# Two-layer recurrent and windowed attention kernel, 16 sequences on one core: the rounded part and the rest of a chunk's decays stacked in one operand, and three steps between stages put elsewhere

## The chip, the cores and the metric

The kernel runs on one core of one Trainium2 chip. The metric is the device time of one execution in microseconds. The kernel before takes 3458.81 us (median of three runs, 3458.78 to 3458.85).

## The reference, cut to what matters

The input is 16 sequences of 1024 tokens with 256 features. Each passes through two layers: `x = x + attention(norm(x)) * silu(ffn(norm(x)))`. The first layer has a gated linear attention (16 heads of 16) and a mixture of 8 experts of which the best 2 count; the second has a windowed attention (64 keys) and a ternary feed-forward network of 1024 hidden units.

The change is in the first attention. Its recurrence is

```python
gk = (jax.nn.log_sigmoid(x @ Wgk1 @ Wgk2 + bgk2) / 16.0).reshape(Bb, Ll, H, Dh)
def step(state, inp):
    qt, kt, vt, gt = inp
    gate = jnp.exp(gt)
    state = state * gate[..., None] + vt[..., None] * kt[..., None, :]
    out_t = jnp.einsum('bhvk,bhk->bhv', state, qt)
    return (state, out_t)
```

The kernel computes it in chunks of 128 tokens, so for each chunk it needs running sums of `gk`, counted from the middle of the chunk (position 64), and the totals of the chunk's first and second half.

## The kernel before, in words

A sequence is 8 chunks of 128 tokens (NC = 8) and two groups of 512 (NG = 2). The 16 sequences are unrolled in one block; each engine runs its own list of instructions in the order of the program and waits on semaphores. `at(name, value)` is a count within the current sequence. A sequence takes some 212 us and goes through these stages:

- **Head.** The head of the next sequence (norm, turned x, low-rank gate input, gate pre-activations) is computed during the feed-forward stage of the current one. `head_rstd` on GpSimd (L367) computes a reciprocal root for four chunks; it waits for `nve_ok`, which VectorE signals after `head_moments`. `head_normalise` on VectorE (L372) follows, and TensorE turns two chunks with `head_turn`.
- **Decays.** ScalarE computes Exp and then Ln of the pre-activations (L890, L899); VectorE forms `gk` for two chunks (L1194) and rounds it to float32r, `gk_hi` (L1198); GpSimd's `decay_low` (L804) subtracts to get the rest, `gk_lo`. TensorE's `cumulate(c)` (L1576, L1577) multiplies three constant 128 by 128 matrices with both parts: six products of 256 columns per chunk, in float32r, which keeps the sums exact enough. `cumulate(0)` stands between `first_queries_keys(6)` and `(7)`; `cumulate(c + 1)` stands in chunk c between `experts_up(c, 1)` and the products with the state (L1713). ScalarE's `decays(c)` takes three Exp of the sums (L924, L928, L933). `parity_scores(c)` on TensorE (L1619) waits for the last of them.
- **SP's queue.** SyncE loads x (8 transfers, L744, after the outputs of the sequence before have landed), then for each group writes the gate rows to DRAM (L749), waits until they have landed, and loads them back spread over 128 partitions as `g_wide` (L755, two transfers of 512 KB).
- **GpSimd's queue.** `parity_queries(0)`, the four `decay_low`, then `hidden_gated(0)` (L819), which waits for `g_wide`, then for each chunk the mask of the state (L839), `parity_queries(c + 1)` (L776) and `hidden_gated(c + 1)`. TensorE's `experts_up(c, 0)` (L1647) waits for `hidden_gated(c)`.
- **Chunks of the first attention.** Per chunk: scores (L1619), values and gates (L1508), `experts_up` (L1647, L1650), `cumulate(c + 1)`, then, after VectorE's masked scores (`causal_scores`, L1245), the products of L1713 and L1719, the turned output, the state's product (L1733) and, in chunks 0 to 3, `experts_down` (L1549).
- **Windowed attention.** Per chunk: masks (L1768), scores (L1781), turned probabilities (L1798), values (L1816), their turn (L1825). For parts 2 and 3 `window_values` on TensorE (L1756) reuses a bank half that VectorE's `attention_bias` (L1415) reads, and waits for it. VectorE's order is row maxima (L1378), shifted scores (L1387) for each of four score banks, then `attention_bias(c - 1)`, then `attention_out(c)`.
- **Feed-forward.** 16 steps n: products of L1879 and L1884, relu on ScalarE (L1113), the square on GpSimd (L867), rounding on ScalarE (L1092), the rest on VectorE (L1470), and `project(n - 3)` on TensorE (L1897), which waits for that rest. GpSimd's `head_rstd` follows its squares 4 and 7; VectorE's `head_normalise` runs in its steps 6 to 9.

## Time and profile before

| | |
|---|---|
| median of three runs | 3458.81 us |
| the profiled execution's own time | 3460.7 us |
| its span | 3459.0 us |
| TensorE matmul busy | 3342.5 us, 97% |
| VectorE, ScalarE, GpSimd busy | 75%, 54%, 37% |
| the chain that ended last: TensorE, VectorE, ScalarE, issue | 75%, 12%, 5%, 5% |
| mean granted TensorE clock | 0.997 |

The span runs from the first to the last instruction; the execution's own time is 1.7 us longer. "Issue" in the chain is time in which the engine waited for nothing that the profile shows. In a timeline, the bracket behind a row is the engine's idle time before it and who ended it; a row of the chain of waits has a start, a length and a name. Matmul ends in a timeline are modelled, so consecutive matmuls overlap by about 0.16 us there; starts are the better measure.

### The profile page before, as it was taken

To read this page: it belongs to the slowest core of one execution; us is meant where nothing else is said; L and a number is where in the kernel's file an instruction comes from. 1 tells how busy PE (TensorE), PEld (TensorE's weight loads), DVE (VectorE), ACT (ScalarE), POOL (GpSimd) and SP (SyncE) were. 2 spreads that over 40 slices of the span, in tenths; PEclk is the share of its full clock that TensorE was granted. 3 is DMA by queue.
4 is the path that set the end of the run, shared out by engine and by line. 5 is a ranking of instruction groups with operands and counts; after the bars stand their busy time and mean duration, and the time that the engine had idled before them with its cause. 6 is when DMAs were issued, how large, how long until landed. Compare 5 with 4: busy or idle time off the path is not lost.

```text
span 3459.0 us, 88576 instructions
## 1 busy us (share of the span) xinstructions
PE 3342.5 (97%) x34556; PEld 2274.0 (66%) x34556; DVE 2607.4 (75%) x6329; ACT 1863.8 (54%) x4135; POOL 1273.4 (37%) x1393
## 2 busy tenths in 40 slices
PE   6999999999999999999999999999999999999998
PEld 3676666766666666666666666666676666766666
DVE  6777867778677777877778777786777867778777
ACT  3364654646546465463655636456364653646546
POOL 4424244242442524325233342423434244242442
PEclk8999999999999999999999999999999999999999
DMA  4001010010110101011010100101001010010110
GB/s 105 18 22 47 24 38 19 24 44 24 38 23 24 40 24 47 14 38 26 24 50 11 50 18 20 49 12 49 18 23 45 24 38 23 20 44 24 38 23 26
DMA packets 98479, 109.59 MB, mean 32 GB/s; under 512 B 21153, under 2 KB 75025, under 8 KB 98065
## 3 DMA queue, kind: packets, MB, share of 16 engines
q1 hardware_dynamic: 93200, 102.25, 11.3%
q8 instruction: 276, 4.52, 0.5%
q10 hardware_dynamic: 4864, 1.69, 0.2%
q14 instruction: 139, 1.13, 0.1%
HBM read 74.01 MB, written 17.30 MB: 26 GB/s over the span
## 4 chain that ended last, share of the span: by engine, by line
PE 75%; DVE 12%; ACT 5%; issue 5%; POOL 1%; DMA 0%; DVEq 0%; SPq 0%; ACTq 0%; POOLq 0%
PE bank L1549 6%; PE bank L1508 5%; PE bank L1879 5%; PE bank L1647 5%; PE bank L1529 5%; PE bank L1781 5%; PE bank L1897 4%; PE bank L1719 4%; PE bank L1664 3%; PE bank L1619 3%; PE bank L1816 3%; PE bank L1842 3%; PE bank L1604 3%; PE bank L1713 2%; DVE am L1245 2%
## 5 line engine op out<-in xcount | busy, mean ns | idle before, releaser
L867 POOL TENSOR_TENSOR qx<-qx 128x512 f32<-128x512 f32 x256 | 277.3, 1088 | 658.7 <-ACT qx L1113 657.8
L1470 DVE TENSOR_TENSOR sq_lo<-qx,sq_hi 128x512 fp32r<-128x512 f32 x256 | 224.1, 875 | 177.1 <-ACT sq_hi L1092 176.6
L1378 DVE TENSOR_REDUCE row_max<-bank 128x4 f32<-128x384 f32 x512 | 270.8, 550 | 95.4 <-PE bank L1781 95.0
L1245 DVE TENSOR_TENSOR am<-bank,causal 128x512 f32<-128x512 f32 x512 | 328.1, 683 | 11.3 <-PE bank L1619 11.3
L988 ACT ACTIVATE tanh_g<-bank 128x256 f32<-128x256 f32 x128 | 49.3, 385 | 394.9 <-PE bank L1508 394.9
L1508 PE MATMUL bank<-w_vg,xt 128*128 128x512 f32 x512 | 252.3, 615 | 0.0
L1549 PE MATMUL bank<-xt,w_down 128*128 128x512 f32 x512 | 237.2, 596 | 0.0
L1897 PE MATMUL bank<-sq_hi,pj_t 128*128 128x512 f32 x512 | 213.2, 416 | 14.8 <-DVE sq_lo L1470 10.3
L1387 DVE TENSOR_TENSOR am<-bank,row_max 128x384 f32<-128x384 f32 x384 | 212.8, 554 | 9.8
L1113 ACT ACTIVATE qx<-bank,scale_fc 128x512 f32<-128x512 f32 x256 | 177.9, 695 | 70.9 <-PE bank L1884 69.0
L1032 ACT ACTIVATE am<-am 128x384 f32<-128x384 f32 x384 | 202.9, 528 | 8.5 <-DVE am L1387 8.5
L1897 PE MATMUL bank<-sq_lo,pj_t 128*128 128x512 f32 x512 | 202.7, 396 | 0.0
L776 POOL TENSOR_TENSOR qx<-qt,par_mask 128x512 f32<-128x512 f32 x128 | 136.3, 1065 | 164.7 <-ACT qt L453 148.4
L1092 ACT CAST sq_hi<-qx 128x512 fp32r<-128x512 f32 x256 | 159.0, 621 | 55.8 <-POOL qx L867 52.8
L1304 DVE TENSOR_TENSOR state_sum<-bank,state_mid 128x256 f32<-128x256 f32 x112 | 47.4, 423 | 176.5 <-PE bank L1733 176.5
L785 POOL TENSOR_SCALAR o_veps<-o_mom 128x1 f32<-128x1 f32 x128 | 38.0, 297 | 367.3 <-DVE o_mom L1325 367.3
L1879 PE MATMUL bank<-xh,fc_t 128*128 128x512 f32 x512 | 171.9, 416 | 0.0
L1781 PE MATMUL bank<-k,qt 32*32 32x192 f32 x8192 | 164.5, 332 | 4.6 <-ACT qt L966 4.6
L1798 PEld LDWEIGHTS bank<-ident,am 64*96 64x96 f32 x4096 | 130.1, 123 | 58.6 <-issue 26.9
L1798 PE MATMUL bank<-ident,am 64*96 64x64 f32 x4096 | 166.9, 221 | 0.0
L1619 PE MATMUL bank<-qx,k 32*128 32x256 f32 x2048 | 146.6, 400 | 15.4 <-issue 12.1
L1879 PE MATMUL bank<-xl,fc_t 128*128 128x512 f32 x512 | 159.9, 393 | 0.0
(264 smaller groups left out, 8671.4 us busy)
## 6 DMA issues: line engine op xcount, KB each, us to landing
g_wide<-gate_rows SPq DMA_DIRECT2D x64, 512.0 KB, 6.0
x<-in_L_attn_x SPq DMA_DIRECT2D x128, 128.0 KB, 2.3
qt<-in_L_attn_x SPq DMA_DIRECT2D x128, 128.0 KB, 2.6
out<-x SPq DMA_DIRECT2D x128, 128.0 KB, 1.7
k<-k SPq DMA_DIRECT2D x96, 128.0 KB, 2.4
qt<-in_L_attn_x ACTq DMA_DIRECT2D x8, 128.0 KB, 7.6
x<-in_L_ffn_w_fc SPq DMA_DIRECT2D x1, 1024.0 KB, 5.9
attn<-in_L_ffn_w_proj SPq DMA_DIRECT2D x1, 1024.0 KB, 8.7
```

The source lines that it names most:

```text
L867: nc.gpsimd.tensor_tensor(sq[:, n % 3, :], relu[:, n % 3, :], relu[:, n % 3, :], ALU.mult)\
L1245: nc.vector.tensor_tensor(am_tiles[:, :, j], bank[3 + j][:].rearrange("p (f e t) -> p f e t", f=2, e=2), causal[:].unsqueeze(1).unsqueeze( ...
L1378: nc.vector.tensor_reduce(row_max[:, j, :], bank[1 + j][:, 0:4 * KW].rearrange("p (h k) -> p h k", k=KW), AX.X, ALU.max, negate=(j == 0)). ...
L1387: nc.vector.tensor_tensor(pr[:, j], bank[1 + j][:, 0:4 * KW].rearrange("p (h k) -> p h k", k=KW), row_max[:, j, :].unsqueeze(2).broadcast_ ...
L1470: nc.vector.tensor_tensor(sq_lo[:, n % 3, :], sq[:, n % 3, :], sq_hi[:, n % 3, :].bitcast(F32), ALU.subtract)\
L1508: mm = nc.tensor.matmul(dst, xt[:, k, c * P:(c + 1) * P], w[:, k, :], start=(k == 0), stop=(k == KD - 1))
L1549: mm = nc.tensor.matmul(bank[5 if g else j][:], w_down[:, k, j * P:(j + 1) * P], xt[:, k, g * 512:(g + 1) * 512], start=(k == 0), stop=(k ...
L1619: mm = nc.tensor.matmul(bank[3 + j][:, half * 2 * P:(half + 1) * 2 * P], kt[rows, half, c * P:(c + 1) * P], qp[rows, c % 2, half], start=T ...
L1781: mm = nc.tensor.matmul(bank[1 + j][b * WB:(b + 1) * WB, t * 2 * KW:(t + 1) * 2 * KW], q2[rows, t, first:first + WB], k2[rows, :, first:fi ...
L1798: mm = nc.tensor.transpose(bank[5 + r][0:KW, h * QB:(h + 1) * QB], pr[rows, 2 * p + h // 4, h % 4, :], ident[rows, rows])
L1879: nc.tensor.matmul(h_bank, fc_t[:, k, m * P:(m + 1) * P], t[:, g, k, :], start=(t is xh and k == 0), stop=False)
L1897: mm = nc.tensor.matmul(bank[5 + o][:], pj_t[:, m, o * P:(o + 1) * P], part[:, n % 3, :], start=(m == 0 and part is sq_hi), stop=(m == MT ...
```

## The change

The two operands of `cumulate` are built anew. `gk_first` holds, for a chunk, the rounded decays of its first 64 tokens in partitions 0 to 63 and their rests in partitions 64 to 127; `gk_second` holds the rests of the second 64 tokens in partitions 0 to 63 and the rounded ones in 64 to 127. Three constant matrices stand in `cumulator`: one for the first half, one for the second, and all ones. The running sum is the first matrix with `gk_first` plus the second with `gk_second`; the half totals are all ones with either. That is four products per chunk instead of six.

To get there, VectorE still writes the rounded part into `gk_first` (all 128 partitions), GpSimd writes the rest into `gk_low` (the tile `xn`, where it wrote float32r into `xl` before), and three transfers from SBUF to SBUF per pair of chunks, issued by SyncE, move the halves (`decay_moves`): 64 partitions of 2 KB each, twelve per sequence. The third of a pair waits for the first to land. `decay_moves(0)` stands between the loads of x and the first gate rows, those for pairs 1 to 3 between the two groups' gate transfers. `cumulate(c)` waits for the transfers of its pair.

The other parts: ScalarE takes one Exp of a single column into a new tile `warm` between `experts_relu(2)` and `(3)`; VectorE's `attention_bias(c - 1)` stands ahead of the last row maximum for c = 1 and 2; GpSimd's `head_rstd` follows its squares 5 and 8 in place of 4 and 7; VectorE's `head_normalise` pairs run in steps 6, 7, 9 and 10 in place of 6 to 9. The constants' preparation on GpSimd before the first sequence changes with the matrices. Declarations of `warm`, `gk_low = xn` and the renamed constants, and two renamed uses of `gk_hi`, are left out of the diff below.

```diff
@@ -174,8 +175,8 @@
     xh = sb("xh", [P, NG, KD, 512], F32R)
     xl = sb("xl", [P, NG, KD, 512], F32R)
 
-    gk_hi = xh[:].rearrange("p g k t -> p (g k t)").rearrange("p (c d) -> p c d", d=D)
-    gk_lo = xl[:].rearrange("p g k t -> p (g k t)").rearrange("p (c d) -> p c d", d=D)
+    gk_first = xh[:].rearrange("p g k t -> p (g k t)").rearrange("p (c d) -> p c d", d=D)
+    gk_second = xl[:].rearrange("p g k t -> p (g k t)").rearrange("p (c d) -> p c d", d=D)
     q2 = qt
     x_next = qt[:].rearrange("p k t -> p (k t)").rearrange("p (c d) -> p c d", d=D)
     am_flat = am[:].rearrange("p h t -> p (h t)")
@@ -290,9 +292,10 @@
              "st2 ve2 rs2 xn2_ok xt2p_ok xt2_ok qk2p_ok qk2_ok low_ok kh_ok kd_ok v2p_ok v2_ok sc_ok max_ok sub_ok "
              "pr_ok ptp_ok pt_ok ptd_ok pv_ok oc_ok xp_ok rden_ok o2_ok o2tp_ok o2t_ok s2p_ok s2_ok xh_ok xl_ok tp_ok thi_ok tst_ok h2p_ok "
              "relu_ok sq_ok sqh_ok sql_ok pj_ok ft_ok ftp_ok tf2_ok f3_ok f4_ok y2_ok gkh_ok gkl_ok nst_ok nve_ok nrs_ok "
-             "nxn_ok hqp_ok hqk_ok").split()
+             "nxn_ok hqp_ok hqk_ok gkm_ok gkd_ok").split()
     s = {n: sem(n) for n in names}
     out_parts = (bank[6][:, 0:D], bank[1][:, D:2 * D])
+    normalise_steps = (6, 7, 9, 10)
     turn_steps = (MT + 2, MT + 3, MT + 5, MT + 6)
     pair_turn_banks = (2, 1, 3)
     turn_banks = {6: 7, 7: 0}
@@ -322,9 +325,9 @@
             (17, "top_ok"),
             (24, "pt_ok sub_ok"),
             (32, "gw_ok pr_ok am_ok max_ok at_ok sc_ok ptp_ok"),
-            (64, "gl_ok"),
+            (64, "gkm_ok gl_ok"),
             (96, "kd_ok"),
-            (128, "xc_ok"),
+            (128, "xc_ok gkd_ok"),
     ):
         per_sequence.update((name, count) for name in signals.split())
 
@@ -508,9 +511,9 @@
                 link(nc.gpsimd.affine_select(out=tile, in_=tile, compare_op=ALU.is_ge, fill=BIG, base=WIN - 1,
                                              pattern=[[-1, width]], channel_multiplier=1))
 
-            for t in (ident, second_half, xt2, k2, w_low, low_t, gates):
+            for t in (ident, cum_first, cum_second, xt2, k2, w_low, low_t, gates):
                 link(nc.gpsimd.memset(t[:], 0.0))
-            for t in (causal, first_half):
+            for t in (causal, all_ones):
                 link(nc.gpsimd.memset(t[:], 1.0))
             nc.gpsimd.memset(minus_half[:], -0.5).then_inc(cleared, 1)
             link(nc.gpsimd.affine_select(out=ident[:], in_=ident[:], compare_op=ALU.not_equal, fill=1.0, base=0,
@@ -521,11 +524,13 @@
                 head_rstd(pool, part)
             link(nc.gpsimd.affine_select(out=causal[:], in_=causal[:], compare_op=ALU.is_ge, fill=0.0, base=0,
                                          pattern=[[1, P]], channel_multiplier=-1))
-            link(nc.gpsimd.tensor_copy(cum_mid[:], causal[:]))
-            link(nc.gpsimd.tensor_scalar(cum_mid[0:QB, :], cum_mid[0:QB, :], -1.0, None, ALU.add))
-            link(nc.gpsimd.memset(first_half[QB:P, :], 0.0))
-            link(nc.gpsimd.memset(second_half[QB:P, :], 1.0))
-            for i, t in enumerate((cum_mid, first_half, second_half)):
+            link(nc.gpsimd.memset(cum_second[:, QB:P], 1.0))
+            for half in range(2):
+                rows = slice(half * QB, (half + 1) * QB)
+                for t, cols, fill in ((cum_first, slice(0, QB), -1.0), (cum_second, slice(QB, P), 0.0)):
+                    link(nc.gpsimd.affine_select(out=t[rows, cols], in_=t[rows, cols], compare_op=ALU.is_ge, fill=fill,
+                                                 base=0, pattern=[[1, QB]], channel_multiplier=-1))
+            for i, t in enumerate((cum_first, cum_second, all_ones)):
                 link(nc.gpsimd.tensor_copy(cumulator[:, i, :], t[:]))
             link(nc.gpsimd.memset(pick[:], 0.0))
             for r in (0, 2):
@@ -744,7 +749,24 @@
                         sp.dma_start(x[:, c, :], x_dram[bass.ds(seq * NC + c, 1), :, :].rearrange("o p d -> (o p) d"))\
                           .then_inc(s["xc_ok"], 16)
 
+                    def decay_moves(i):
+
+                        two, low, high = slice(2 * i, 2 * i + 2), slice(0, QB), slice(QB, P)
+                        sp.wait_ge(s["gkh_ok"], at("gkh_ok", i + 1))
+                        sp.dma_start(gk_second[high, two, :].bitcast(F32), gk_first[high, two, :].bitcast(F32))\
+                          .then_inc(s["gkm_ok"], 16)
+                        sp.wait_ge(s["gkl_ok"], at("gkl_ok", i + 1))
+                        if i:
+                            sp.wait_ge(s["gkd_ok"], at("gkd_ok", 32 * i))
+                        sp.dma_start(gk_second[low, two, :].bitcast(F32), gk_low[high, two, :]).then_inc(s["gkd_ok"], 16)
+                        sp.wait_ge(s["gkm_ok"], at("gkm_ok", 16 * (i + 1)))
+                        sp.dma_start(gk_first[high, two, :].bitcast(F32), gk_low[low, two, :]).then_inc(s["gkd_ok"], 16)
+
+                    decay_moves(0)
                     for g in range(NG):
+                        if g:
+                            for i in range(1, NC // 2):
+                                decay_moves(i)
                         sp.wait_ge(s["gx_ok"], at("gx_ok", g + 1))
                         sp.dma_start(gate_dram[g], gate_rows[8:8 + E, g * 512:(g + 1) * 512]).then_inc(s["gw_ok"], 16)
                         sp.wait_ge(s["gw_ok"], at("gw_ok", 16 * (g + 1)))
@@ -801,8 +823,8 @@
 
                     def decay_low(i):
                         pool.wait_ge(s["gkh_ok"], at("gkh_ok", i + 1))
-                        nc.gpsimd.tensor_tensor(gk_lo[:, 2 * i:2 * i + 2, :], gk[:, 2 * i:2 * i + 2, :],
-                                                gk_hi[:, 2 * i:2 * i + 2, :].bitcast(F32), ALU.subtract)\
+                        nc.gpsimd.tensor_tensor(gk_low[:, 2 * i:2 * i + 2, :], gk[:, 2 * i:2 * i + 2, :],
+                                                gk_first[:, 2 * i:2 * i + 2, :].bitcast(F32), ALU.subtract)\
                           .then_inc(s["gkl_ok"], 1)
 
                     def rstd2(part, lo, hi):
@@ -866,8 +888,8 @@
                             pool.wait_ge(s["sql_ok"], at("sql_ok", n - 2))
                         nc.gpsimd.tensor_tensor(sq[:, n % 3, :], relu[:, n % 3, :], relu[:, n % 3, :], ALU.mult)\
                           .then_inc(s["sq_ok"], 1)
-                        if n in (4, 7):
-                            head_rstd(pool, n // 7)
+                        if n in (5, 8):
+                            head_rstd(pool, n // 8)
                 now["copy"] = 0
 
             @block.scalar
@@ -915,6 +937,7 @@
                         act.wait_ge(s["gtp_ok"], at("gtp_ok", b + 1))
                         nc.scalar.copy(gate_rows[:, b * 512:(b + 1) * 512], bank[gate_banks[b]][32:64, :]).then_inc(s["gx_ok"], 1)
                     experts_relu(2)
+                    nc.scalar.activation(warm[:], gdiff[:, 0:1], ACT.Exp)
                     experts_relu(3)
                     def decays(c):
 
@@ -1427,9 +1450,11 @@
                         shifted(4 * c + 5)
                         maxima(4 * c + 6)
                         shifted(4 * c + 6)
+                        if 0 < c < 3:
+                            attention_bias(c - 1)
                         maxima(4 * c + 7)
                         shifted(4 * c + 7)
-                        if c:
+                        if c >= 3:
                             attention_bias(c - 1)
                         attention_out(c)
                         if c < 3:
@@ -1479,9 +1504,10 @@
                                 head_stats(dve, c)
                         if n == 3:
                             head_moments(dve)
-                        if 6 <= n < 10:
-                            head_normalise(dve, 2 * (n - 6))
-                            head_normalise(dve, 2 * (n - 6) + 1)
+                        if n in normalise_steps:
+                            p = normalise_steps.index(n)
+                            head_normalise(dve, 2 * p)
+                            head_normalise(dve, 2 * p + 1)
                         if n == NG * MT - 2:
                             head_low_split(dve, 1)
                     finish2(3)
@@ -1566,15 +1592,17 @@
                     experts_down(3)
                     def cumulate(c):
 
-                        pe.wait_ge(s["gkl_ok"], at("gkl_ok", c // 2 + 1))
+                        pe.wait_ge(s["gkd_ok"], at("gkd_ok", 32 * (c // 2 + 1)))
                         if c == 0:
                             pe.wait_ge(s["qk_ok"], at("qk_ok", 3))
                             pe.wait_ge(s["hr_ok"], at("hr_ok", 4))
                         else:
                             pe.wait_ge(s["am_ok"], at("am_ok", 4 * c - 2))
-                        for i, out in enumerate((bank[3][:, 0:D], bank[4][:, 0:D], bank[4][:, D:2 * D])):
-                            nc.tensor.matmul(out, cumulator[:, i, :], gk_hi[:, c, :], start=True, stop=False)
-                            mm = nc.tensor.matmul(out, cumulator[:, i, :], gk_lo[:, c, :], start=False, stop=True)
+                        first, second = gk_first[:, c, :], gk_second[:, c, :]
+                        nc.tensor.matmul(bank[3][:, 0:D], cumulator[:, 0, :], first, start=True, stop=False)
+                        nc.tensor.matmul(bank[3][:, 0:D], cumulator[:, 1, :], second, start=False, stop=True)
+                        nc.tensor.matmul(bank[4][:, 0:D], cumulator[:, 2, :], first, start=True, stop=True)
+                        mm = nc.tensor.matmul(bank[4][:, D:2 * D], cumulator[:, 2, :], second, start=True, stop=True)
                         mm.then_inc(s["cum_ok"], 1)
 
                     first_queries_keys(6)
```

## Rows read from the trace of the kernel before

**Rows 1.** The page's chain that ended last, by engine.
```profile
PE 75%; DVE 12%; ACT 5%; issue 5%; POOL 1%; DMA 0%; DVEq 0%; SPq 0%; ACTq 0%; POOLq 0%
```

**Rows 2.** Chain of waits, start of the seventh sequence's first attention: start us, us, what.
```profile
1346.87 0.12 PE bank L1576
...
1349.31 0.75 issue
```

**Rows 3.** Timeline of SyncE's queue, same stretch: start us, us, operation.
```profile
1337.49 3.66 SPq L744 DMA_DIRECT2D x<-in_L_attn_x  x8
1342.10 0.29 SPq L749 DMA_DIRECT2D gate_rows<-low_t  x1
1343.72 1.28 SPq L755 DMA_DIRECT2D g_wide<-gate_rows  x2
```

**Rows 4.** The page's DMA issues: size, median us from issue to landing.
```profile
x<-in_L_attn_x SPq DMA_DIRECT2D x128, 128.0 KB, 2.3
...
k<-k SPq DMA_DIRECT2D x96, 128.0 KB, 2.4
```

**Rows 5.** Timelines of GpSimd and TensorE, same stretch.
```profile
1351.25 1.28 POOL L819 TENSOR_TENSOR qx<-qx,g_wide 128x512 f32<-128x512 f32 x1 [4.62 <-DMA g_wide<-gate_rows]
...
1353.17 1.89 PE L1647 MATMUL bank<-w_up,qx 128*128 128x256 f32 x8
```

**Rows 6.** Timelines of SyncE, GpSimd, TensorE where the fourteenth sequence starts its first attention.
```profile
2829.42 1.28 SPq L755 DMA_DIRECT2D g_wide<-gate_rows  x2
...
2837.05 1.27 POOL L819 TENSOR_TENSOR qx<-qx,g_wide 128x512 f32<-128x512 f32 x1 [5.79 <-DMA g_wide<-gate_rows]
...
2838.37 1.99 PE L1647 MATMUL bank<-w_up,qx 128*128 128x256 f32 x8 [0.43 <-POOL qx L819]
```

**Rows 7.** Windows, fourteenth and fifteenth sequence: us, busy per engine, PEclk, DMA, GB/s.
```profile
2834.67:3047.37 212.70, 207.59 (x2155) 141.02 (x2155) 160.51 (x389) 115.62 (x258) 77.81 (x82) 1.00 0.12 31
3047.37:3259.33 211.96, 207.27 (x2154) 140.98 (x2155) 160.51 (x388) 115.59 (x258) 77.79 (x82) 1.00 0.12 30
```

**Rows 8.** Timeline of TensorE's weight loads in chunk 1; groups by line, whole span.
```profile
1365.95 0.52 PEld L1713 LDWEIGHTS bank<-qt,state_mid 128*128 128x128 f32 x4 [0.20 <-DVE am L1245]
...
L1713 PEld LDWEIGHTS bank<-qt,state_mid 128*128 128x128 f32 x512 | 67.2, 190 | 26.8 <-DVE am L1245 25.9
```

**Rows 9.** Timeline of ScalarE, same stretch as Rows 2.
```profile
1347.51 1.28 ACT L924 ACT_TABLE_LOAD   x1
1348.81 0.39 ACT L924 ACTIVATE decay_in<-bank 128x256 f32<-128x256 f32 x1
```

**Rows 10.** Timelines of TensorE and VectorE in the windowed attention.
```profile
1246.22 0.65 PE L1756 MATMUL bank<-ident,low_t 64*96 64x64 f32 x8 [0.28 <-DVE attn L1415]
...
1245.75 0.41 DVE L1415 TENSOR_TENSOR attn<-bank,bc_o 128x256 f32<-128x256 f32 x1
...
1248.34 1.02 DVE L1378 TENSOR_REDUCE row_max<-bank 128x4 f32<-128x384 f32 x2 [0.41 <-PE bank L1781]
```

**Rows 11.** Timelines of GpSimd and TensorE in the feed-forward stage.
```profile
1294.11 1.40 POOL L367 TENSOR_TENSOR rstd<-veps,minus_half 128x4 f32<-128x4 f32 x1 [3.35 <-DVE veps L361]
1295.47 2.04 POOL L867 TENSOR_TENSOR qx<-qx 128x512 f32<-128x512 f32 x2
...
1294.43 0.63 PE L1879 MATMUL bank<-xh,fc_t 128*128 128x512 f32 x2
...
1296.52 0.62 PE L1879 MATMUL bank<-xh,fc_t 128*128 128x512 f32 x2
...
1299.15 0.62 PE L1879 MATMUL bank<-xh,fc_t 128*128 128x512 f32 x2
```

**Rows 12.** Windows in the kernel's prologue; columns as in Rows 7.
```profile
51.70:53.70 2.00, 0.00 (x0) 0.00 (x0) 0.00 (x0) 2.00 (x4) 0.00 (x0) 1.00 0.00 0
53.80:56.10 2.30, 0.00 (x0) 0.00 (x0) 0.00 (x0) 0.56 (x3) 0.01 (x1) 0.50 0.03 7
56.20:60.50 4.30, 4.30 (x5) 1.79 (x6) 2.84 (x13) 2.72 (x6) 0.94 (x1) 0.50 0.75 193
```

More of the change, by code:

```diff
@@ L113, in build_program @@
     gden = sb("gden", [P, NC])
+    warm = sb("warm", [P, 1])
     g_top = sb("g_top", [P, 2, NC])
@@ L205, in build_program @@
     z, zact, gk = am_flat.rearrange("p (c d) -> p c d", d=D), xn, attn2
+    gk_low = xn
     u_nat = am_flat[:, 0:MT * RANK].rearrange("p (m r) -> p m r", m=MT)
@@ L212, in build_program @@
     b_nat = am_flat[:, 3 * D + 3 * P:4 * D + 3 * P]
-    cum_mid, first_half, second_half = (am_flat[:, 3 * D + i * P:3 * D + (i + 1) * P] for i in range(3))
+    cum_first, cum_second, all_ones = (am_flat[:, 3 * D + i * P:3 * D + (i + 1) * P] for i in range(3))
     fc_nat, pj_ter = x, kt
@@ L1197, in _ @@
                         dve.wait_ge(s["gk_ok"], at("gk_ok", i + 1))
-                        nc.vector.tensor_copy(gk_hi[:, two, :], gk[:, two, :]).then_inc(s["gkh_ok"], 1)
+                        nc.vector.tensor_copy(gk_first[:, two, :], gk[:, two, :]).then_inc(s["gkh_ok"], 1)
                     dve.wait_ge(s["xc_ok"], at("xc_ok", 16 * NC))
```

## The prediction

> **What bounds the kernel now.** I read the chain of waits first: three quarters of it is TensorE [rows 1], so at most places an edit is worth what it takes off TensorE's own list, unless TensorE stands waiting there. So I went through one sequence of 212 us looking for the places where it waits, and asked at each edit which wait ends last. Four places matter.
>
> At the start of the first attention, the six products of `cumulate(0)` start at 1346.87, 0.12 us each; after the next projection TensorE waits 0.75 us for the three Exp of ScalarE [rows 2]. Ahead of them ScalarE loads its Exp table, 1.28 us, after the Ln table of the decays [rows 9].
>
> SyncE's queue is in order: x until 1341.15, gate rows at 1342.10, `g_wide` at 1343.72 once those landed [rows 3]. GpSimd waits for `g_wide` until 1351.25, works 1.28 us, and TensorE's `experts_up(0)` starts at 1353.17 without a wait [rows 5]. The slack is 1353.17 - 1352.53, about 0.6 us.
>
> How a late `g_wide` passes on can be read in the fourteenth sequence. There it is issued 5.25 us ahead of the scores (2829.42 against 2834.67) and not 6.34 us (1343.72 against 1350.06), so 1.09 us late; `experts_up` starts 3.70 us after the scores and not 3.11, so 0.59 us late [rows 2, 3, 5 to 7]. That sequence is 0.74 us longer than the next [rows 7]: nothing later gives the delay back, and some 0.15 us of it are weight loads that are no longer hidden.
>
> In the chunks, the products with the state (L1713) stand behind `cumulate(c + 1)` and behind VectorE's masked scores. In chunk 1 their weight load waits for VectorE, and over the span these waits come to 25.9 us [rows 8]. Where VectorE ends last, shorter sums only lengthen that wait.
>
> **The change part by part.**
>
> *Two products fewer per chunk.* 2 x 0.12 = 0.24 us of TensorE [rows 2], for 128 chunks 30.7 us if all of it counted. It counts in `cumulate(1)`, which stands in chunk 0 where TensorE has its own work and no wait for VectorE: 0.24 us. In chunks 1 to 6 VectorE's scores end at nearly the same moment or later [rows 8]; I take 0.1 us for all of them together, between 0 and 6 x 0.24 = 1.44. `cumulate(0)` stands ahead of a stall that comes below, so its 0.24 us are worth nothing. Sum: -0.34 us per sequence.
>
> *The Exp into `warm`.* It pulls the table load of 1.28 us [rows 9] ahead to where ScalarE waits between two relus. By itself that removes the 0.75 us of [rows 2], with the 0.24 us of `cumulate(0)` 0.99 us. This too lies ahead of the stall below. Price taken: 0, between -0.99 and +0.3 us (ScalarE's next relu comes a little later, and `cumulate(0)` waits for it). The row shows no drain: the load takes 1.28 us and the next activation starts 0.02 us after it [rows 9]. The Trainium skill, page "ScalarE: Activation LUTs", section "What ACT_TABLE_LOAD costs", adds about 1.38 us of drain to each load, 2.66 us in all; by that the load would reach into the next relu and delay `cumulate(0)` by over 1 us, which the stall would hide here as well.
>
> *The moves on SyncE's queue.* This is the term that decides. `decay_moves(0)` stands ahead of the gate rows. The first move is issued at 1341.15, directly behind x [rows 3]. A move has the size of the key moves, 128 KB, whose median is 2.4 us from issue to landing [rows 4]; so it lands at 1343.55 at the earliest, and as it queues behind the loads of x, which take 2.3 us themselves with the last issued at about 1340.7 [rows 3, 4], I take 1344.0. SyncE waits for that before it issues the third move. With 0.6 us for its issue (an estimate: a `g_wide` takes 1.28 / 2 [rows 3]) the gate rows go out at 1344.6 in place of 1342.10. They needed 1.62 us to land and now stand behind the third move, which lands at 1344.0 + 2.4 = 1346.4. So `g_wide` goes out at 1346.4 in place of 1343.72: 2.7 us late (between 1.75 and 3.7). GpSimd then starts `hidden_gated(0)` at 1353.95, ends at 1355.23, and TensorE starts `experts_up(0)` at 1355.28, which is 2.1 us late; with the 0.15 us of exposed loads +2.25 us. What queues behind on GpSimd (the state's mask, the queries and `hidden_gated` of chunk 1) has several microseconds of room, since TensorE needs it only in chunk 1. `cumulate(0)` itself needs the third move at 1346.4 and would start at 1346.87: just in time, and hidden by the stall if not. The moves of pairs 1 to 3 are issued behind `g_wide`; they are needed first by chunk 1's sums, just ahead of 1365.95 [rows 8], and the second group's gates wait for chunk 3 anyway: 0. The Trainium skill, page "DMA: Bandwidth & Descriptors", section "Queues, rings and completion order", says that each DMA engine consumes a queue's descriptors in the order of the ring; by that rule the 2.7 us stand, and without it 2.05 us would do.
>
> *The clock.* TensorE would now be ready for `experts_up(0)` at 1353.17 - 0.99 = 1352.2 and stand until 1355.28, some 3.1 us. In the prologue it stood from about 51.7; the granted clock was 1.00 until 53.7, 0.50 (1.2 in place of 2.4 GHz) from 53.8, and the work after the stop ran at 0.50 for 4.3 us [rows 12]. A stop of over 2.1 us can thus bring the clock down. No stop in the sequences of the trace is that long. At half rate 4.3 us of work lose 2.15 us; a shorter stop may lose less or nothing. I take 1.1 us per sequence, half of it, between 0 and 2.15.
>
> *`attention_bias` earlier for c = 1 and 2.* `window_values` waits 0.28 us for it [rows 10], twice per sequence, and 0.07 us of weight loads are exposed each time. The bias takes a slot of some 0.4 us and now precedes a maximum and a subtraction, so it ends about 1 us earlier and the wait goes. VectorE's next maxima had 0.41 us of idle time ahead [rows 10], so it can follow. -2 x 0.35 = -0.70 us (between 0 and -0.7; the next wait would be VectorE's own list).
>
> *`head_rstd` one square later.* GpSimd waits 3.35 us for VectorE's variances, takes 1.40 us, and only then squares step 5, at 1295.47, though its input is long there. TensorE's step is 1299.15 - 1296.52 = 2.63 us there, where a free one is 1296.52 - 1294.43 = 2.09 us [rows 11]. One square later, step 5 passes ahead of that wait: -0.54 us (between 0 and -0.54). `head_normalise` in steps 9 and 10 is work off the path, needed by TensorE four steps later: 0.
>
> *The constants* before the first sequence: a few small GpSimd instructions, 0, within 1 us.
>
> **The sum.** Per sequence +2.25 - 0.34 - 0.70 - 0.54 = +0.67 us, with the clock +1.77 us; times 16, +28.3 us. The profiled execution took 3460.7 us for a span of 3459.0, so it would take 3489.0; the median of the runs is 1.9 us below that execution, so 3487.
>
> **The rivals.**
>
> *The clock holds.* The same stall, but 3.1 us don't bring the clock down: +10.7 us, 3469.5. For it: only the prologue shows falls, in stops of over 4 us. Against: the fall came some 2.1 us into the stop [rows 12].
>
> *The first move lands fast.* If it lands 2.4 us after its issue and nothing holds the gate rows behind the third, `g_wide` is 2.05 us late, `experts_up(0)` 1.46 + 0.15 = 1.61 us, and the gains of 1.58 us cancel it: 3459. With an issue of 0.3 us `g_wide` is 1.75 us late and the kernel takes 3454. The point of sign is a gate write at 1344.2.
>
> *The other side: the gates are not held up.* Place: the wait ahead of the third move. If the moves land so soon, or x is so early, that `g_wide` goes out within 0.5 us of its old time, `warm` pays: `experts_up(0)` is then bound by GpSimd at 1352.58, 0.59 us earlier, and the sequence gains 0.59 + 0.34 + 0.70 + 0.54 = 2.17 us: 3424. It decides from `g_wide` less than 2.0 us late downward. Against it: a transfer's latency stands in the queue, which nothing here shortens.
>
> *Worse.* Every sequence loses the full 2.15 us to the clock, and in some the loads of x land late, 1 us more: 0.67 + 2.15 = 2.82 us, 3504 and above.
>
> *The change doesn't do what it says* if the table is loaded again for `decays(0)`; hidden by the stall, it would show only in the third rival, as +0.75 us per sequence.
>
> **How the numbers follow.** Forecast with the clock falling 0.41; clock holds 0.17; fast move 0.20; gates not held up 0.14; worse 0.08. The range from 3448 to 3504 leaves out the fourth and half of the last. A measurement of this kernel can tell 0.2%, 7 us, from no change. Faster than 3451.9: the fourth case and 0.05 of the third, 0.19. Within 7 us: 0.15 of the third and, with a gain or a delay a little off, 0.05 of the second, 0.20. Slower: 0.61.
>
> **What would show it.** In the profile after: four sum products per chunk; `g_wide` issued some 2.7 us later relative to the projection ahead of it; GpSimd's wait for `g_wide` about 7 us in place of 4.6; TensorE waiting some 3 us for `hidden_gated(0)` ahead of L1647, 50 us in all; the table load between two relus and no wait ahead of the scores; granted clock under 0.99 in the mean with half-rate stretches behind that stop; no wait of L1756 for the bias; an even step of 2.09 us in the feed-forward stage. The prediction is wrong if L1647 doesn't wait, if `g_wide` is under 2 us late, or if the sums' reduction is worth 0.24 us in every chunk because VectorE's scores come earlier too.

## The result, and the profile after

The changed kernel takes 3494.76 us (median of four runs, 3490.67 to 3504.48), against 3458.8 us before: a ratio of 1.0109 (95% interval 1.0088 to 1.013), about 36 us slower. The forecast was 3487. The profiled execution took 3493.8 us, at a mean granted clock of 0.991 against 0.997 before.

The page of the changed kernel: span, busy times, the shares of the chain, the costliest group that is new, and the medians from issue to landing of the three moves.

```profile
span 3491.5 us, 88324 instructions
...
PE 3333.0 (95%) x34300; PEld 2259.5 (65%) x34300; DVE 2594.6 (74%) x6329; ACT 1864.6 (53%) x4151; POOL 1267.7 (36%) x1395
...
PE 69%; DVE 14%; DMA 6%; ACT 5%; issue 3%; SPq 1%; POOL 1%; DVEq 0%; ACTq 0%; POOLq 0%
...
L1675 PE MATMUL bank<-w_up,qx 128*128 128x256 f32 x512 | 135.8, 413 | 55.5 <-POOL qx L841 55.5
...
xl<-xh SPq DMA_DIRECT2D x64, 128.0 KB, 2.4
xl<-xn SPq DMA_DIRECT2D x64, 128.0 KB, 2.4
xh<-xn SPq DMA_DIRECT2D x64, 128.0 KB, 2.2
```

TensorE has 256 matmuls fewer and is busy 9.5 us less, yet the span is 32.5 us longer. Transfers, which held nothing of the chain before [rows 1], hold 6% of it. One group explains it: `experts_up` (L1675, before L1647) now waits 55.5 us for GpSimd's `hidden_gated`. Its mean of 413 ns is the second sign: in a kernel with no stop there it is 381 (`e4_three_seams` below), so part of it runs at the lower clock.

The same place as [rows 2, 3, 5, 9], in the seventh sequence; the scores start at 1360.15 here, where they started at 1350.06 before. Timeline of SyncE's queue:

```profile
1348.07 3.66 SPq L749 DMA_DIRECT2D x<-in_L_attn_x  x8
1351.78 0.53 SPq L756 DMA_DIRECT2D xl<-xh  x1
1352.36 1.58 SPq L761 DMA_DIRECT2D xl<-xn  x1
1355.51 0.46 SPq L763 DMA_DIRECT2D xh<-xn  x1
1356.02 0.48 SPq L771 DMA_DIRECT2D gate_rows<-low_t  x1
1358.00 1.30 SPq L777 DMA_DIRECT2D g_wide<-gate_rows  x2
1359.35 0.61 SPq L756 DMA_DIRECT2D xl<-xh  x1
```

From the first load of x it is 7.95 us to the gate rows and 9.93 to `g_wide`; before it was 4.61 and 6.23 [rows 3]. The hole ahead of 1355.51 is the wait for the first move: it was issued at 1351.78 and landed 3.72 us later. The chain of waits of the same stretch says it in four lines:

```profile
1351.78 3.72 DMA xl<-xh
...
1355.51 0.46 SPq L763
...
1356.02 1.97 DMA gate_rows<-low_t
...
1358.69 7.37 DMA g_wide<-gate_rows
```

Timelines of ScalarE, TensorE and GpSimd there:

```profile
1354.76 1.28 ACT L940 ACT_TABLE_LOAD   x1
1356.05 0.20 ACT L940 ACTIVATE warm<-gdiff 128x1 f32<-128x1 f32 x1
...
1357.76 0.39 PE L1602 MATMUL bank<-xh,cumulator 128*128 128x256 f32 x1 [0.31 <-DMA xh<-xn]
...
1360.15 1.15 PE L1647 MATMUL bank<-qx,k 32*128 32x256 f32 x16
...
1367.50 3.78 PE L1675 MATMUL bank<-w_up,qx 128*128 128x256 f32 x8 [4.07 <-POOL qx L841]
...
1366.19 1.26 POOL L841 TENSOR_TENSOR qx<-qx,g_wide 128x512 f32<-128x512 f32 x1 [8.98 <-DMA g_wide<-gate_rows]
```

The table load has gone to where ScalarE had time, and the wait ahead of the scores is gone with it. But GpSimd waits 8.98 us for `g_wide` in place of 4.62 [rows 5], TensorE stands for 4.07, and the eight products of `experts_up`, 1.89 us before, take 3.78. Windows around the stop show why (columns as in [rows 7]), and below them the seventh and the eighth sequence, the second without a half-rate stretch:

```profile
1361.00:1363.20 2.20, 2.20 (x14) 0.96 (x6) 1.89 (x3) 0.15 (x1) 0.00 (x0) 1.00 0.94 223
1363.40:1367.40 4.00, 0.03 (x1) 0.00 (x0) 1.35 (x3) 0.49 (x2) 1.21 (x1) 0.90 0.55 111
1367.60:1371.00 3.40, 3.40 (x9) 2.76 (x9) 0.00 (x0) 0.00 (x0) 2.75 (x3) 0.50 0.62 143
1374.50:1380.00 5.50, 5.29 (x30) 2.80 (x30) 2.40 (x7) 0.96 (x2) 0.92 (x2) 1.00 0.02 3
1360.15:1576.49 216.34, 208.38 (x2140) 141.38 (x2139) 159.75 (x389) 115.78 (x260) 77.36 (x82) 0.98 0.15 38
1576.49:1789.15 212.66, 205.52 (x2140) 139.21 (x2139) 159.76 (x389) 115.63 (x260) 77.45 (x82) 1.00 0.15 38
```

The granted clock falls to 0.50 (1.2 in place of 2.4 GHz) late in the stop and is 1.00 again by 1374.50. Eleven of the sixteen sequences have such a fall; one of the other five is the first, whose stop is only 0.65 us long. The eighth has none, and is still 0.70 us longer than the 211.96 of [rows 7].

What became of the smaller waits, from the groups by line of the changed kernel:

```profile
L1741 PEld LDWEIGHTS bank<-qt,state_mid 128*128 128x128 f32 x512 | 69.7, 197 | 45.0 <-DVE am L1268 42.1
L1784 PE MATMUL bank<-ident,low_t 64*96 64x64 f32 x512 | 41.5, 221 | 0.0
L370 POOL TENSOR_TENSOR rstd<-veps,minus_half 128x4 f32<-128x4 f32 x34 | 47.8, 1405 | 30.2 <-DVE veps L364 30.2
```

`window_values` (L1784, before L1756) waits for nothing. The weight load of the products with the state (L1741, before L1713) stands 45.0 us in all, mostly for VectorE's scores, in place of 26.8 [rows 8]: much of what TensorE saves on the sums it then waits. GpSimd's wait for the variances is 30.2 us; in the kernel before it was

```profile
L367 POOL TENSOR_TENSOR rstd<-veps,minus_half 128x4 f32<-128x4 f32 x34 | 47.7, 1404 | 59.0 <-DVE veps L361 59.0
```

### The profile page after: what moved, and what is told of

The parts are those of the page before. It is cut to its first block, busy times and chain, and to the rows that moved or that the text cites. A ratio compares the mean times of both kernels' runs of the same rounds, so it can differ in the third digit from the quotient of the medians.

```text
span 3491.5 us, 88324 instructions
## 1 busy us (share of the span) xinstructions
PE 3333.0 (95%) x34300; PEld 2259.5 (65%) x34300; DVE 2594.6 (74%) x6329; ACT 1864.6 (53%) x4151; POOL 1267.7 (36%) x1395
## 4 chain that ended last, share of the span: by engine, by line
PE 69%; DVE 14%; DMA 6%; ACT 5%; issue 3%; SPq 1%; POOL 1%; DVEq 0%; ACTq 0%; POOLq 0%
PE bank L1907 6%; PE bank L1925 5%; PE bank L1809 4%; PE bank L1534 4%; DVE am L1268 4%; PE bank L1844 4%; PE bank L1747 4%; PE bank L1870 4%; PE bank L1675 4%; PE bank L1575 3%; DMA g_wide<-gate_rows 3%; PE bank L1692 3%; PE bank L1632 3%; PE bank L1647 2%; PE bank L1826 2%
## 5 line engine op out<-in xcount | busy, mean ns | idle before, releaser
L1495 DVE TENSOR_TENSOR sq_lo<-qx,sq_hi 128x512 fp32r<-128x512 f32 x256 | 236.5, 924 | 175.6 <-ACT sq_hi L1115 175.1
L1055 ACT ACTIVATE am<-am 128x384 f32<-128x384 f32 x384 | 202.4, 527 | 11.1 <-DVE am L1410 8.5
L1675 PE MATMUL bank<-w_up,qx 128*128 128x256 f32 x512 | 135.8, 413 | 55.5 <-POOL qx L841 55.5
L1025 ACT ACTIVATE tanh_f<-bank 128x256 f32<-128x256 f32 x128 | 49.2, 385 | 251.7 <-PE bank L1678 251.7
L1826 PEld LDWEIGHTS bank<-ident,am 64*96 64x96 f32 x4096 | 129.9, 123 | 58.4 <-issue 26.8
```

Source lines behind the costliest of these rows:

```text
L1495: nc.vector.tensor_tensor(sq_lo[:, n % 3, :], sq[:, n % 3, :], sq_hi[:, n % 3, :].bitcast(F32), ALU.subtract)\
L1675: nc.tensor.matmul(bank[up_banks[c]][:, 0:D], hidden_t[c // 4][:, j, c % 4 * P:(c % 4 + 1) * P], w_up[:, j, :], start=(j == 0), stop=False)
L1826: mm = nc.tensor.transpose(bank[5 + r][0:KW, h * QB:(h + 1) * QB], pr[rows, 2 * p + h // 4, h % 4, :], ident[rows, rows])
```

## The experiments

Ten kernels ran, each beside the kernel before (3458.9 us). The heading says whether a kernel starts from the changed one ("after") or from the unchanged one ("before"). Three dots in a diff stand for lines left out.

**e1_no_moves: after, without the moves.** GpSimd writes the rests straight into the second operand and nothing is rearranged, so the running sums are wrong; only the time of this kernel is of use.

```diff
-                    decay_moves(0)
...
-                        if g:
-                            for i in range(1, NC // 2):
-                                decay_moves(i)
...
-                        nc.gpsimd.tensor_tensor(gk_low[:, 2 * i:2 * i + 2, :], gk[:, 2 * i:2 * i + 2, :],
+                        nc.gpsimd.tensor_tensor(gk_second[:, 2 * i:2 * i + 2, :], gk[:, 2 * i:2 * i + 2, :],
...
-                        pe.wait_ge(s["gkd_ok"], at("gkd_ok", 32 * (c // 2 + 1)))
+                        pe.wait_ge(s["gkl_ok"], at("gkl_ok", c // 2 + 1))
```

> The changed kernel without its transfers: GpSimd writes the rests in float32r straight into the second operand, nothing is moved between the partitions, and the four products and the three moved steps stay. It leaves out the rearrangement of the operands, so its running sums are not the reference's. My theory (the wait ahead of the third move holds up the gates): the gates go out at their old time, no long stop ahead of experts_up(0), granted clock at 0.997 again, 3424 us (3416 to 3432). Rival 1, that the gates were not the cause (something else in the first attention is slower): it stays above 3470. Rival 2, that two products fewer count in every chunk: 0.24 us in six chunks more, 3401.

Measured 3418.76 us (ratio to before 0.9885, 0.9868 to 0.9901), clock 0.997. From the groups by line:

```profile
L1658 PE MATMUL bank<-w_up,qx 128*128 128x256 f32 x512 | 122.6, 382 | 1.0 <-POOL qx L824 0.9
L1724 PEld LDWEIGHTS bank<-qt,state_mid 128*128 128x128 f32 x512 | 66.8, 190 | 45.2 <-DVE am L1251 42.1
```

The twelve transfers per sequence cost 76.0 us: without them the stop is 1.0 us in place of 55.5 and nothing in the sixteen sequences runs at half rate. All that the change could win stands here too: 40 us against the kernel before. The wait for VectorE (45.2 us) is the same with and without the moves, so it belongs to the shorter sums.

**e2_third_behind: after, with the third move of pair 0 and the wait ahead of it behind the issue of the first gate rows.** The first and second moves stay where they are; `last_move(i)` is that wait with the third move of pair i.

```diff
                     decay_moves(0)
                     for g in range(NG):
...
                         sp.dma_start(gate_dram[g], gate_rows[8:8 + E, g * 512:(g + 1) * 512]).then_inc(s["gw_ok"], 16)
+                        if g == 0:
+                            last_move(0)
                         sp.wait_ge(s["gw_ok"], at("gw_ok", 16 * (g + 1)))
```

> The changed kernel with one thing moved: the third move of pair 0 (and the wait ahead of it) stands behind the issue of the first gate rows instead of ahead of it. My theory: the gate rows go out right behind the second move, g_wide still waits for the third move's issue, so it is about 1.2 us later than in the kernel before relative to the scores, experts_up(0) stops some 1.8 us in place of over 3, and the clock falls seldom: 3448 us (3443 to 3458). Rival, that the bandwidth or the number of the transfers and not the order of the queue holds up the gates: above 3480, as the changed kernel.

Measured 3449.49 us (0.9973, 0.9963 to 0.9984), clock 0.996. SyncE's queue in the seventh sequence (scores at 1342.55), and the group of `experts_up`:

```profile
1334.76 0.53 SPq L756 DMA_DIRECT2D xl<-xh  x1
1335.33 0.59 SPq L761 DMA_DIRECT2D xl<-xn  x1
1335.97 0.50 SPq L777 DMA_DIRECT2D gate_rows<-low_t  x1
1337.78 0.46 SPq L769 DMA_DIRECT2D xh<-xn  x1
1338.28 1.30 SPq L785 DMA_DIRECT2D g_wide<-gate_rows  x2
...
L1683 PE MATMUL bank<-w_up,qx 128*128 128x256 f32 x512 | 126.4, 391 | 26.9 <-POOL qx L849 26.9
```

The same twelve transfers, with one wait of SyncE and the move behind it at another place, are 45.3 us cheaper. The gate rows go out 4.92 us after x's first load (1331.05) in place of 7.95. What is left of the stop, 26.9 us, has three sources: TensorE itself is ready 1.0 us earlier than before (scores 11.46 us after x's first load in the mean, before 12.48), `g_wide` still stands behind the third move and its wait (in the mean it goes out 7.12 us after x's first load, before 6.15), and in the mean it takes 8.03 us from its issue to GpSimd's start in place of 7.61, with moves of pair 1 issued behind it.

**e3_late_gates: before, with two moves between idle tiles ahead of the gate rows, the second waiting for the first to land.** Nothing else of the change is in it.

```diff
+                    sp.dma_start(sq_hi[QB:P, 0, :].bitcast(F32), w_vg[QB:P, 0, :]).then_inc(s["sa_ok"], 16)
+                    sp.wait_ge(s["sa_ok"], at("sa_ok", 16))
+                    sp.dma_start(sq_lo[0:QB, 0, :].bitcast(F32), sq_hi[QB:P, 0, :].bitcast(F32)).then_inc(s["sb_ok"], 16)
...
+                            pe.wait_ge(s["sb_ok"], at("sb_ok", 16))
```

> The kernel before with nothing of the change but the delay: two chained transfers of 64 partitions of 2 KB between tiles that are idle there, the second waiting for the first to land, stand on SyncE's queue ahead of the first gate rows, and cumulate(0) waits for the second. Six products, nothing else moved. My theory: g_wide about 3 us late, experts_up(0) 2.5 us late and 0.15 us of exposed loads, 42 us for 16 sequences; the stop of TensorE is 2.5 us, and the clock falls in some of them, 5 to 15 us more: 3508 us (3498 to 3520). Rival 1, a late g_wide is absorbed: 3459 to 3470. Rival 2, the clock costs nothing: 3501 with a granted clock of 0.997.

Measured 3505.42 us (1.0132, 1.0115 to 1.0149), clock 0.993; `experts_up` waits 33.9 us. The delay of the gates by itself, with six products and the old seams, costs 46.5 us, the clock's falls in seven sequences of its profile included. It is slower than the changed kernel, and it has none of its gains.

**e4_three_seams: before, with `warm`, the bias and the `rstd` steps, and nothing of the sums.**

```diff
-                        if n in (4, 7):
-                            head_rstd(pool, n // 7)
+                        if n in (5, 8):
+                            head_rstd(pool, n // 8)
...
+                    nc.scalar.activation(warm[:], gdiff[:, 0:1], ACT.Exp)
...
+                        if 0 < c < 3:
+                            attention_bias(c - 1)
                         maxima(4 * c + 7)
                         shifted(4 * c + 7)
-                        if c:
+                        if c >= 3:
                             attention_bias(c - 1)
...
-                        if 6 <= n < 10:
+                        if n in (6, 7, 9, 10):
```

> The kernel before with the three moved steps and the early Exp, but with its six products and without any transfer. My theory: early Exp 0.59 us per sequence (then GpSimd's hidden_gated(0) ends last), the bias 0.70, the reciprocal roots 0.54: 1.83 us times 16 = 29 us, 3429.5 us (3424 to 3437); that leaves 5 us between it and the kernel without moves for the shorter sums. Rival, that the three hide behind one another or behind VectorE: 3445 or more. Rival 2, sums count everywhere: the distance to the kernel without moves is 28 us or more.

Measured 3426.36 us (0.9905, 0.9889 to 0.9922), clock 0.996:

```profile
L1652 PE MATMUL bank<-w_up,qx 128*128 128x256 f32 x512 | 121.8, 381 | 0.6 <-POOL qx L820 0.6
L1718 PEld LDWEIGHTS bank<-qt,state_mid 128*128 128x128 f32 x512 | 66.9, 190 | 26.9 <-DVE am L1247 25.7
```

Three small edits take 32.5 us off, and the wait for VectorE is that of before. Since e1 is e4 with shorter sums, their difference is what four products in place of six are worth: 7.6 us, with 30.7 us of products removed (256 x 0.12). Some of it may be the start and not the sums: in the two profiles the first scores stand at 75.09 (e1) and 76.86 (e4), and from there to the scores of the sixteenth sequence the gain is 0.41 us per sequence. This is the fastest kernel here that computes the whole, 68.4 us below the changed one.

**e7_warm_only, e5_bias_only, e6_rstd_only: before, with one of those three edits each** (the lines are those of e4; e6 has both `head_rstd` and `head_normalise`).

> The kernel before with the early Exp alone. My theory of the prediction: 0.75 us of TensorE's wait goes, GpSimd's hidden_gated(0) then ends last, 0.59 us per sequence, 3449.4 us. After the run of the three seams together (3426.4, 32.5 us faster), where experts_up(0) started without a wait, rather the full 0.75 to 0.8 us: 3446 (3444 to 3450). Rival, that the load ahead of the relu delays cumulate(0): 3455 or more.

> The kernel before with the bias ahead of the last maximum for c = 1 and 2 alone. Theory: 2 x 0.35 us per sequence, 3447.6 us (3446 to 3450). Rival, that VectorE's own list takes the place of the wait: 3455 or more.

> The kernel before with the reciprocal roots one square later and the normalised pairs in steps 6, 7, 9, 10, alone. Theory: 0.54 us per sequence, 3450.2 us (3448 to 3453). Rival, that the normalised pairs come too late for TensorE's turns: 3459 or more.

Measured: `warm` 3448.09 us (0.9966, 0.9952 to 0.9979), the bias 3447.77 (0.9966, 0.9952 to 0.9979), the `rstd` steps 3448.51 (0.997, 0.9959 to 0.9981), that is 10.8, 11.1 and 10.4 us less than before, 32.3 together; e4 has 32.5, so they add up. Each one's own wait in the groups by line, first the scores of `warm`, then `window_values` of the bias, then GpSimd's step of `rstd`:

```profile
L1621 PE MATMUL bank<-qx,k 32*128 32x256 f32 x2048 | 146.7, 400 | 3.3 <-ACT attn L908 3.3
...
L1758 PE MATMUL bank<-ident,low_t 64*96 64x64 f32 x512 | 41.5, 221 | 0.0
...
L367 POOL TENSOR_TENSOR rstd<-veps,minus_half 128x4 f32<-128x4 f32 x34 | 47.6, 1402 | 30.7 <-DVE veps L361 30.7
```

and the first two in the kernel before:

```profile
L1619 PE MATMUL bank<-qx,k 32*128 32x256 f32 x2048 | 146.6, 400 | 15.4 <-issue 12.1 <-ACT attn L907 3.3
L1756 PE MATMUL bank<-ident,low_t 64*96 64x64 f32 x512 | 41.5, 221 | 9.1 <-DVE attn L1415 9.1
```

The wait of 12.1 us ahead of the scores is the 0.75 of [rows 2] sixteen times, and `warm` turns 10.8 of it into time. In the changed kernel it does away with the same wait, and by the trace the stop takes it back; the changed kernel without `warm` was not run.

**e9_filled_stop and e10_filled_less: after, with unused products in the stop**, ten and six of them, ahead of the first `experts_up` of each sequence. They work on data that is there, so that TensorE does not stand idle.

```diff
+                            if c == 0:
+                                for i in range(6):
+                                    nc.tensor.matmul(bank[2][:, 0:D], xt[:, i % 2, 0:P], w_vg[:, i % 2, 0:D],
+                                                     start=True, stop=True)
```

> The changed kernel with ten products of 256 columns, 2.2 us of TensorE, whose results nothing reads, ahead of the wait of experts_up(0). They lie within a stop that is over 3 us long in all sequences but the first. My theory, that the clock costs about 1.1 us per sequence: the granted clock stays at 0.997, nothing else changes, 3475 us (3468 to 3483). Rival, that the fallen clock costs nothing because other engines or the late gates set the end: 3494 or, with the fill, more.

Measured 3485.76 us (1.0077, 1.0062 to 1.0092), clock 0.998: a miss by 11 us. A product of these float32 operands is two instructions, so ten took 4.48 us in the seventh sequence, more than the stop: `experts_up` has no wait left (0.0) and starts 7.43 us after the scores in the mean, later than the 6.94 of the changed kernel. e10 repeats it with six.

> As the filled stop, with six products in place of ten. The ten were 20 instructions and took 4.3 us, not 2.2, longer than the stop: experts_up(0) started 7.43 us after the scores in every sequence, 0.48 us later than the mean of the changed kernel, which by itself is some 8 us. Six take 2.6 us and lie within the stop. My theory: clock 0.997, experts_up(0) where it was, 3475 us (3470 to 3480), so 20 us of the changed kernel are the clock's. Rival, the clock costs 9 us, as the difference to the ten products says: 3486.

Measured 3478.02 us (1.0054, 1.004 to 1.0068), clock 0.997:

```profile
L1679 PE MATMUL bank<-w_up,qx 128*128 128x256 f32 x512 | 122.6, 382 | 15.2 <-POOL qx L841 15.2
```

`experts_up` starts as late as in the changed kernel (6.88 us after the scores in the mean), but no stretch of the sixteen sequences runs at half rate. So the clock costs 16.7 us of the changed kernel's time, 1.05 us per sequence; 13.2 of them are in this one group (135.8 against 122.6). The figure is good to a few us only, since the four times of the changed kernel spread over 14 us; the two profiled executions differ by 14.0. The rest of the loss, 19.2 us over before, is the delay alone less the gains.

**e8_second_rounding: e2, with VectorE rounding the upper half a second time straight into `gk_second`.** Four products as in the change, but in pair 0 no move waits for another; the moves of pairs 1 to 3 still wait for those of the pair before.

```diff
                         nc.vector.tensor_copy(gk_first[:, two, :], gk[:, two, :]).then_inc(s["gkh_ok"], 1)
+                        nc.vector.tensor_copy(gk_second[QB:P, two, :], gk[QB:P, two, :]).then_inc(s["gkm_ok"], 1)
...
-                        sp.dma_start(gk_second[high, two, :].bitcast(F32), gk_first[high, two, :].bitcast(F32))\
-                          .then_inc(s["gkm_ok"], 16)
...
-                        sp.wait_ge(s["gkm_ok"], at("gkm_ok", 16 * (i + 1)))
```

> Four products with the transfers kept, but no transfer waits for another: VectorE rounds the second half's decays a second time, straight into the second operand (64 partitions, four more instructions), so the first move and the wait behind it go; of pair 0 the one move is issued ahead of the first gate rows, the other behind their issue. Theory: the gate rows go out at most 0.6 us late, g_wide stands behind 128 to 256 KB of moves, experts_up(0) stops about 1 us, the clock stays: 3432 us (3424 to 3440), so faster than the kernel before but not than the three seams alone with six products (3426). Rival, that the bandwidth of the moves holds up the gates more: 3445 or more.

Measured 3435.02 us (0.9931, 0.9916 to 0.9946), clock 0.996; `experts_up` waits 14.8 us. It is 59.7 us faster than the changed kernel and 8.7 slower than e4: the transfers still cost more than the 7.6 us of the shorter sums. Against e1, which has no transfers, it is 16.3 us slower: so much they cost with no wait between the moves ahead of the gates.

## Why the prediction was right, step by step

The sign, the mechanism and the place were right, and the time lay in the range. The steps against the runs, in us per sequence; times from x's first load are means over the sequences 2 to 16 (in the first, x is there long before, and nothing is late):

| step of the prediction | predicted | measured |
|---|---|---|
| `g_wide` issued later | 2.7 | 2.98 (9.13 against 6.15 after x) |
| `experts_up(0)` later | 2.1 | 2.82 (18.46 against 15.64 after x) |
| TensorE's stop in all | 50 us | 55.5 us |
| the clock | 1.1 | 1.05 (e10) |
| products with the shorter sums | -0.34 | -0.475 (e1 against e4; -0.41 behind the first scores), 0.1 of it at `cumulate(0)` |
| bias | -0.70 | -0.69 (e5) |
| `rstd` | -0.54 | -0.65 (e6) |
| `warm` in the change | 0 | not measured apart, 0 by the trace; -0.67 alone (e7) |

**The moves.** Two runs show the cause from both sides: taking the moves away gives 76 us (e1), and putting two such moves alone into the kernel before costs 46.5 (e3). e2 pins it on the third move and the wait ahead of it, as the prediction had it; in the seventh sequence the wait lasts until 1355.51, and the move's own issue takes 0.5 us after that. The gate rows go out 7.14 us after x's first load in the mean, and 7.11 were predicted (1344.6 less 1337.49); the first move takes 2.87 us in the mean where 2.85 was taken, though 3.72 in the seventh sequence. The mis-sized term is what follows, and it makes the delay of `experts_up` 0.7 us too small. First, the gate rows landed 1.99 us after their issue where 1.8 was taken; with that and a mean of 6.15 in place of 6.23 before, `g_wide` is 0.28 us later than predicted. Second, a term that the prediction put at 0, the moves issued behind `g_wide`: `hidden_gated(0)` starts 8.02 us after the issue of `g_wide` in the mean, in the kernel before 7.61, and in e3, where the gates are as late but no moves stand behind them, 7.64. Against e1, which is this kernel without moves, the difference is larger (7.32). The window from 1361.00 shows the transfer engines 94% busy. With 2.98 + 0.41 us and the slack of 0.6, 2.8 us come out, as measured.

The Trainium skill, page "DMA: Bandwidth & Descriptors", section "Queues, rings and completion order", says that each DMA engine takes a queue's descriptors in the order of the ring, though a later one may finish its write before an earlier one. The landings here came in the order of issue, which agrees with it and doesn't prove it: the gate rows, issued at 1356.02 behind the third move, landed at 1357.99, the third move, for which `cumulate(0)` waited, just before 1357.76.

**The clock.** The mean was right by luck: 1.1 us was half of an upper bound, with no row for the half. The picture behind it, half of a full loss in every sequence, was not what the trace shows: in eleven sequences a fall, in five none. The length of the stop doesn't sort them. There were falls where `experts_up` started 6.11 and 6.34 us after the scores (stops of 2.83 and 3.06 us), and none at 6.54, 6.61, 6.64 and 6.72 us (stops of 3.26 to 3.44). The prediction read from the prologue that a stop of over 2.1 us can bring the clock down; in e3 a stop of 1.87 us did (ninth sequence, below: TensorE's row behind the stop, and two windows), and one of 3.21 us did not (fourth).

```profile
1805.01 3.26 PE L1652 MATMUL bank<-w_up,qx 128*128 128x256 f32 x8 [1.87 <-POOL qx L823]
...
1802.10:1805.50 3.40, 1.53 (x6) 0.76 (x5) 2.13 (x5) 0.65 (x2) 1.82 (x2) 1.00 0.06 10
1805.60:1808.90 3.30, 3.30 (x11) 2.77 (x10) 0.00 (x0) 0.39 (x1) 2.25 (x3) 0.50 0.00 0
```

So the rival that the clock holds is out, and a kernel with this stop can land a few us either side. Its four executions fit that: 3490.67 and 3493.8 us at a mean clock of 0.991, 3495.72 at 0.989, 3504.48 at 0.988.

**The shorter sums.** Right in kind: a quarter of the 30.7 us arrives (7.6), because VectorE's scores end last in most chunks. L1713's wait grows by 18.2 us (45.0 against 26.8; 18.3 in e1 against e4). Of the 0.475 us per sequence 0.1 lie at `cumulate(0)`, where the change gets nothing for them (`experts_up(0)` starts 14.74 us after x in e1 and 14.84 in e4); the other 0.375, or 0.31 counted behind the first scores, stand against the 0.34 predicted.

**The small steps.** The bias was right to 0.01 us. With `rstd` the step from 1296.52 to 1299.15 [rows 11] became an even 2.09 us, and the stage as a whole gained 0.1 more. By the trace it was right to count `warm` for nothing here: the scores start 0.95 us earlier after x (11.53 against 12.48; 0.99 predicted, 0.24 of it `cumulate(0)`), and the stop is longer by that. Alone it is worth 0.67, a little over the 0.59 of the third rival. The load of 1.28 us shows no drain, as in [rows 9]: the relu ahead of it ends 0.02 us before it, and the activation starts 0.01 us behind it.

**The sum.** 2.82 x 15 for the delay, less 0.7 in the first sequence, 41.6 us, the clock 16.7, less 11.1 and 10.4, and less 6 for the sums (7.6 without the 0.1 per sequence of `cumulate(0)`, which lies ahead of the stop): 30.8 us, where the profiled executions differ by 33.1. About 2 us stay unexplained, less than the uncertainty of the clock's term alone; the prediction's 0.15 us of exposed weight loads would be 2.4, and no run shows that term by itself.

Not run: the gate rows ahead of x, and four products in pairs 1 to 3 with six in pair 0, which would leave nothing ahead of the first gates.

## What to carry to other kernels

A queue that issues in order turns a wait for one transfer into a delay of every transfer behind it, also of those that have nothing to do with it: before putting a chain of transfers ahead of another, look for who waits for the other one and how much slack there is (here 0.6 us against a delay of 3). Work taken off the busiest engine pays only where no other engine ends last: of 30.7 us of products 7.6 arrived, while three reordered steps, each chosen at a wait that the timeline named, brought 32.5. When a change bundles gains with one loss, build its parts singly; the parts without the loss may be the better kernel.

## What the runs showed of the hardware

- TensorE's granted clock fell to 0.50 around stops of 1.87, 2.83 and 3.06 us and held through others of 3.21 to 3.44 us (e3 and the changed kernel). All falls of the changed kernel together cost some 16.7 us (e10).
- Filling a stop with unused products keeps the granted clock up (0.997 against 0.991). With a fill shorter than the stop `experts_up` starts as before and 16.7 us are gained (e10); with one longer than the stop it starts 0.5 us later and only 9.0 are gained (e9).
- A float32 product of 256 columns here is two instructions, 0.22 us each (ten products are 20 in 4.48 us, e9); one in float32r is a single instruction of 0.12 us [rows 2].
- A move of 128 KB from SBUF to SBUF lands in 2.2 to 2.4 us in the median, but the first one behind 1 MB of loads took up to 3.72 in the changed kernel. With two moves behind `g_wide`, GpSimd's work on it started 0.41 us later after its issue than in the kernel before, and 0.70 later than in e1.
